# A GRU's hidden product, made block by block inside an earlier sort instead of in the GRU stage

## The reference

```python
feat_in, feat_out = h @ W_in.T + b_in, h @ W_out.T + b_out
a_in = seg_mean(feat_in[src], dst, N)
a_out = seg_mean(feat_out[dst], src, N)
a = concatenate((a_in, a_out), axis=1)
gi, gh = a @ w_ih.T + b_ih, h @ w_hh.T + b_hh     # 3 x 128 columns each: r, z, n
r, z = sigmoid(i_r + h_r), sigmoid(i_z + h_z)
n = tanh(i_n + r * h_n)
h = (1 - z) * n + z * h
x = layernorm(x + h)
```

## Time and profile before

| | |
|---|---|
| median of 3 runs | 14506.02 us |
| lowest and highest | 14486.2, 14518.42 us |
| the profiled execution: its time | 14487.43 us |
| the profiled execution: its span | 14485.9 us |
| mean granted TensorE clock | 0.815 |
| busy share of the span | TensorE 73%, VectorE 52%, ScalarE 27%, GpSimd 68% |
| stage `sort_records` | from 2371 to 6585 us |
| first loop of `node_update` | from 8777 to 9119 us |

### The profile page before, as it was taken

One profiled execution on the slowest core, in us unless ns is written; L12 is line 12 of the kernel. 1 busy time (PEld: TensorE's weight loads), 2 busy tenths in 40 slices (PEclk: granted clock), 3 DMA queues, 4 the chain that ended last, 5 costly groups with the idle time before them and its releaser, 6 DMA issues. The chain is left out here.

```text
span 14485.9 us, 317356 instructions
## 1 busy us (share of the span) xinstructions
PE 10556.1 (73%) x72077; PEld 8423.3 (58%) x72078; DVE 7488.2 (52%) x28446; ACT 3839.8 (27%) x10046; POOL 9837.9 (68%) x10445
## 2 busy tenths in 40 slices
PE   3666665666666666666777768689999999999961
PEld 2444444555555555555777765467777767777751
DVE  5444444333333333336777765356656656556644
ACT  0000001222222222220000004355555555555530
POOL 4777775777777777777777770267777767777740
PEclk8555556777787777788999989599999999999975
DMA  6722222333333333336777771133333353333351
GB/s 202 273 55 55 55 55 70 107 106 107 107 106 107 106 107 106 107 106 163 187 188 189 188 166 38 34 73 79 80 80 80 80 71 80 80 80 79 80 47 31
DMA packets 2182961, 1488.42 MB, mean 103 GB/s; under 512 B 1344360, under 2 KB 1972744, under 8 KB 2181125
## 3 DMA queue, kind: packets, MB, share of 16 engines
q0 software_dynamic: 387600, 800.47, 20.4%
q1 hardware_dynamic: 1751242, 565.87, 17.1%
q10 hardware_dynamic: 43942, 120.50, 2.3%
HBM read 1117.42 MB, written 480.14 MB: 110 GB/s over the span
## 5 line engine op out<-in xcount | busy, mean ns | idle before, releaser
L1637 POOL DMA_INDIRECT ring<-q_rows,small x3556 | 3360.4, 945 | 1205.2 <-issue 927.9
L992 POOL DMA_INDIRECT edges_a<-ring,small x1664 | 1596.8, 960 | 586.6 <-issue 505.7
L992 POOL DMA_INDIRECT edges_b<-ring,small x1664 | 1596.5, 959 | 507.1 <-issue 504.4
L1124 POOL DMA_INDIRECT ring<-in_x,ring x1664 | 1570.2, 944 | 536.9 <-issue 522.9
L746 POOL DMA_INDIRECT ring<-in_x,ring x1664 | 1570.0, 944 | 530.2 <-issue 487.6
L1677 PE MATMUL bank<-w,ring 64*128 64x129 f32 x7112 | 1743.3, 325 | 127.6 <-DVE ring L1591 105.6
L784 PE MATMUL bank<-ring 128*128 128x129 f32 x3328 | 1281.2, 492 | 758.1 <-DMA ring<-in_x,ring 546.7
L784 PEld LDWEIGHTS bank<-ring 128*128 128x128 f32 x3328 | 827.7, 310 | 1177.3 <-DMA ring<-in_x,ring 585.0
L923 PE MATMUL bank<-ident_b,ring 128*128 128x128 bf16 x3332 | 422.1, 266 | 1480.8 <-DVE ring L878 1480.8
L947 PE MATMUL bank<-p,ring 128*128 x6656 | 1347.0, 366 | 128.3 <-ACT ring L977 80.7
L1677 PEld LDWEIGHTS bank<-w,ring 64*128 64x128 f32 x7112 | 1057.1, 186 | 639.7 <-DVE ring L1591 312.1
(11 more groups left out here) (253 smaller groups left out, 21022.0 us busy)
## 6 DMA issues: line engine op xcount, KB each, us to landing
p<-edges_b SPq DMA_DIRECT2D x525, 262.0 KB
p<-edges_a SPq DMA_DIRECT2D x520, 262.0 KB
ring<-bonds_by_dst SPq DMA_DIRECT2D x3344, 32.0 KB
bonds_by_dst<-in_bond ACTq DMA_DIRECT2D x5, 20625.0 KB, 159.8
ring<-edges_a SPq DMA_DIRECT2D x1792, 33.0 KB
ring<-edges_b SPq DMA_DIRECT2D x1776, 33.0 KB
ring<-q_rows,small POOLq DMA_INDIRECT x3556
ring<-in_x,ring POOLq DMA_INDIRECT x3328
```

The lines of the kernel that those rows point to most:

```text
L992: pool.indirect_dma_start(out=c.edges[s], out_offset=bass.IndirectOffsetOnAxis(ap=pos[:, k:k + 1], axis=0), in_=rec[:, k, :], in_offset=No ...
L1124: pool.indirect_dma_start(out=gath[:, at, 0:D], out_offset=None, in_=c.ins["x"], in_offset=bass.IndirectOffsetOnAxis(ap=ids[g][:, 0, k:k + ...
L1637: pool.indirect_dma_start(out=gath[:, k, 0:D], out_offset=None, in_=c.q_dram, in_offset=bass.IndirectOffsetOnAxis(ap=gidx[g][:, k % HALF:k ...
```

## The change

In turn i of the sort, for i under 98, block i of x is loaded, transposed (TensorE, after quad 2), copied (ScalarE, after quad 3), multiplied by W_hh with the candidate's bias added (TensorE, after quad 4), copied (ScalarE, after quad 6) and stored to memory as 384 columns (SyncE, in group 3 of the turn). In `node_update` the transpose of x, its two products and the `cand` banks go. The stored rows are loaded with x, VectorE adds 256 of their columns to the bank in a new `sum_rz`, the sigmoid reads that sum, and t1 reads the other 128.

```diff
+    s_xb, s_xt, s_xtc, s_hx, s_hxc, s_hxo = (c.sem("r_x_block_in"), c.sem("r_x_turned"), c.sem("r_x_turned_copied"),
...
+    T_X, A_XT, T_HX, A_HX = 2, 3, 4, 6
...
+            def store_hidden(b):
+                sp.wait_ge(s_hxc, b + 1)
+                sp.dma_start(c.hx_dram[bass.ds(b * P, P), :], hx).then_inc(s_hxo, 16)
+
+            def load_x(b):
+                sp.wait_ge(s_xt, b)
+                sp.dma_start(xb, c.x_pad[bass.ds(b * P, P), :]).then_inc(s_xb, 16)
+
+            load_x(0)
+            per = TURNS_R // SPARTS
+            for part, first, last in ((0, 0, per), (1, per, 2 * per), (2, 2 * per, 3 * per), (3, 3 * per, NB - 1),
+                                      (4, NB - 1, NB), (4, NB, TURNS_R)):
+                if 1 <= part < SPARTS:
...
+                with sp.Fori(first, last) as i:
                     for g in range(GRPS):
                         u = i * GRPS + g
+                        if first < NB and g == GRPS - 1:
+                            store_hidden(i)
+                        if first < NB - 1 and g == GRPS - 1:
+                            load_x(i + 1)
                         sp.wait_ge(s_xv, u * 4 + 3)
...
+            def turn_x(b):
+                pe.wait_ge(s_xb, 16 * b + 16)
+                pe.wait_ge(s_xtc, b)
+                nc.tensor.transpose(xt_bank, xb, c.ident).then_inc(s_xt, 1)
+
+            def hidden(b):
+                pe.wait_ge(s_xtc, b + 1)
+                pe.wait_ge(s_hxc, b)
+                nc.tensor.matmul(hx_bank, xt, c.weight(W_HH, 3 * D), start=True, stop=False, skip_group_check=True)
+                nc.tensor.matmul(hx_bank[:, 2 * D:3 * D], c.ones_f[0:1, :], c.rows[0:1, (B_HH + 2) * D:(B_HH + 3) * D],
+                                 start=False, stop=True, skip_group_check=True).then_inc(s_hx, 1)
+
+            pe.wait_ge(c.s_w, 15 * 16)
...
+                for first, last in ((0, TURNS_R // 2),) if s == 0 else ((TURNS_R // 2, NB), (NB, TURNS_R)):
+                    with pe.Fori(first, last) as i:
...
+                            if first < NB and q == T_X:
+                                turn_x(i)
+                            if first < NB and q == T_HX:
+                                hidden(i)
...
+            def copy_x(b):
+                act.wait_ge(s_xt, b + 1)
+                act.wait_ge(s_hx, b)
+                nc.scalar.copy(xt, xt_bank).then_inc(s_xtc, 1)
+
+            def copy_hidden(b):
+                act.wait_ge(s_hx, b + 1)
+                act.wait_ge(s_hxo, 16 * b)
+                nc.scalar.copy(hx, hx_bank).then_inc(s_hxc, 1)
...
+            for first, last in ((0, NB), (NB, TURNS_R)):
...
+                        if first < NB and q == A_XT:
+                            copy_x(i)
+                        if first < NB and q == A_HX:
+                            copy_hidden(i)
...
     xs = [place(D) for _ in range(XSLOTS)]
+    hxs = [c.spare[:, n * 3 * D:(n + 1) * 3 * D] for n in range(XSLOTS)]
     m_in, m_out = ([place(D) for _ in range(2)] for _ in range(2))
-    m_t = [place(3 * P) for _ in range(2)]
+    m_t = [place(2 * P) for _ in range(2)]
+    rz_pre = [place(2 * D) for _ in range(2)]
...
+                sp.dma_start(hxs[n], c.hx_dram[n * P:(n + 1) * P, :]).then_inc(s_in[n], 16)
...
+                sp.dma_start(hxs[j % XSLOTS], c.hx_dram[bass.ds((b + XSLOTS) * P, P), :]).then_inc(s_in[j % XSLOTS], 16)
...
-                n, b, x = j % 2, i * TURN + j, xs[j % XSLOTS]
+                n, b, x, hidden = j % 2, i * TURN + j, xs[j % XSLOTS], hxs[j % XSLOTS]
...
-                step.link(nc.vector.tensor_tensor(t1, cand[n][:, 0:D], rz[n][:, 0:D], ALU.mult))
+                step.link(nc.vector.tensor_tensor(t1, hidden[:, 2 * D:3 * D], rz[n][:, 0:D], ALU.mult))
...
+            def sum_rz(b, j):
+                n = j % 2
+                dve.wait_ge(s_gate, b + 3)
+                dve.wait_ge(s_in[j % XSLOTS], (b - j) // TURN * 64 + 32 * (j // XSLOTS + 1) if isinstance(b, int)
+                            else rz_turn * 64 + 32 * (j // XSLOTS + 1))
+                nc.vector.tensor_tensor(rz_pre[n], gates[n][:, 0:2 * D], hxs[j % XSLOTS][:, 0:2 * D], ALU.add).then_inc(s_rz, 1)
+
+            sum_rz(0, 0)
             with dve.Fori(0, TURNS_N - 1) as i:
                 step.loop(i, 5 * TURN)
                 for j in range(TURN):
+                    rz_turn = i + (j + 1) // TURN
+                    sum_rz(i * TURN + (j + 1), (j + 1) % TURN)
                     gru(i, j)
             step.end(TURNS_N - 1)
             for j in range(TURN):
+                if j + 1 < TURN:
+                    sum_rz((TURNS_N - 1) * TURN + j + 1, j + 1)
                 gru(TURNS_N - 1, j)
...
-                pe.wait_ge(s_in[j % XSLOTS], i * 32 + 16 * (j // XSLOTS + 1))
...
-                nc.tensor.transpose(turned[n][:, 2 * P:3 * P], xs[j % XSLOTS], c.ident)
...
-                in_t, out_t, x_t = (m_t[n][:, k * P:(k + 1) * P] for k in range(3))
+                in_t, out_t = (m_t[n][:, k * P:(k + 1) * P] for k in range(2))
                 nc.tensor.matmul(gates[n][:, 0:3 * D], in_t, c.weight(W_IH1, 3 * D), start=True, stop=False,
                                  skip_group_check=True)
                 nc.tensor.matmul(gates[n][:, 0:3 * D], out_t, c.weight(W_IH2, 3 * D), start=False, stop=False,
                                  skip_group_check=True)
-                nc.tensor.matmul(gates[n][:, 0:2 * D], x_t, c.weight(W_HH, 2 * D), start=False, stop=False,
-                                 skip_group_check=True)
                 nc.tensor.matmul(gates[n][:, 0:3 * D], has_t[n], rows9[:, 0:3 * D], start=False, stop=True,
-                                 skip_group_check=True)
-                nc.tensor.matmul(cand[n][:, 0:D], x_t, c.weight(W_HH + 2), start=True, stop=False)
-                nc.tensor.matmul(cand[n][:, 0:D], has_t[n], rows9[:, 3 * D:4 * D], start=False,
-                                 stop=True).then_inc(s_gate, 1)
+                                 skip_group_check=True).then_inc(s_gate, 1)
 
...
-                nc.scalar.copy(m_t[n], turned[n][:, 0:3 * P]).then_inc(s_tc, 1)
+                nc.scalar.copy(m_t[n], turned[n][:, 0:2 * P]).then_inc(s_tc, 1)
...
-                act.wait_ge(s_gate, b + 3)
-                nc.scalar.activation(rz[n], gates[n][:, 0:2 * D], ACT.Sigmoid).then_inc(s_sig, 1)
+                act.wait_ge(s_rz, b + 1)
+                nc.scalar.activation(rz[n], rz_pre[n], ACT.Sigmoid).then_inc(s_sig, 1)
```

More of the change, by code:

```diff
@@ L183, in __init__ @@
         self.q_dram = dram("q_rows", [NPAD, D])
+        self.hx_dram = dram("hidden_gates", [NPAD, 3 * D])
         self.s_copy = [nc.alloc_semaphore(f"bonds_copied{k}") for k in range(COPIES)]
@@ L805, in sort_records @@
     QUADS, BK1, TURNS_R = DEEP // QUAD, NB + 1, SLOTS // DEEP
+    s_xb, s_xt, s_xtc, s_hx, s_hxc, s_hxo = (c.sem("r_x_block_in"), c.sem("r_x_turned"), c.sem("r_x_turned_copied"),
+                                             c.sem("r_hidden"), c.sem("r_hidden_copied"), c.sem("r_hidden_out"))
+    T_X, A_XT, T_HX, A_HX = 2, 3, 4, 6
     rec = c.part(0, DEEP * REC).rearrange("p (k r) -> p k r", k=DEEP)
@@ L818, in sort_records @@
     junk = c.part(top, QUAD * BK1).rearrange("p (k b) -> p k b", k=QUAD)
-    assert top + QUAD * BK1 <= RINGW
+    top += QUAD * BK1
+    xb, xt, hx = c.part(top, D), c.part(top + D, P), c.part(top + 2 * D, 3 * D)
+    assert top + 5 * D <= RINGW
+    xt_bank, hx_bank = c.bank[5][:, 0:P], c.bank[6][:, 0:3 * D]
     posf = c.small[:, 64:64 + DEEP].rearrange("p (q j) -> p q j", j=QUAD)
@@ L851, in _ @@
                 load_bonds(g, g, 0)
-            for part in range(SPARTS):
-                if part:
+            def store_hidden(b):
[9 more added lines that the diff above has]
+                if 1 <= part < SPARTS:
                     sp.wait_ge(c.s_copy[part + 1], 16)
-                with sp.Fori(part * (TURNS_R // SPARTS), (part + 1) * (TURNS_R // SPARTS)) as i:
+                with sp.Fori(first, last) as i:
                     for g in range(GRPS):
                         u = i * GRPS + g
+                        if first < NB and g == GRPS - 1:
+                            store_hidden(i)
+                        if first < NB - 1 and g == GRPS - 1:
+                            load_x(i + 1)
                         sp.wait_ge(s_xv, u * 4 + 3)
@@ L867, in _ @@
             sp.wait_ge(s_tab, 64)
+            sp.wait_ge(s_hxo, 16 * NB)
         @block.vector
@@ L955, in _ @@
                                  start=True, stop=False, skip_group_check=True)
[L956 to L961, removed]
+                for first, last in ((0, TURNS_R // 2),) if s == 0 else ((TURNS_R // 2, NB), (NB, TURNS_R)):
+                    with pe.Fori(first, last) as i:
+                        for q in range(QUADS):
+                            rank(i, q)
+                            turn_hot(i + (q + 1) // QUADS, (q + 1) % QUADS)
+                            find(i, q)
```

(28 more changed lines are left out.)

## The result

| | before | after |
|---|---|---|
| median | 14500.44 us (4 runs) | 14781.56 us (4 runs) |
| lowest to highest | 14486.2 to 14518.42 | 14779.64 to 14793.73 |
| span of the profiled execution | 14485.9 | 14778.7 |

The ratio is 1.0195, with a 95% interval of 1.0177 to 1.0213: the change makes the kernel 281 us slower.

The account below looks back on a forecast made before the run. GpSimd's scatters were taken to bound the sort, TensorE the GRU blocks. Profiled 14487.4 us + 271 (GRU loop) + 3 (stage start) + 0 (sort) = 14761; as a median, 18.6 us higher, 14780 us; range 14615 to 14830.

Parts of the forecast that it names:

- What left TensorE: GRU blocks: a transpose and three products go, 1.21 us a block; 119 us only if TensorE stayed the bound.
- The chain: GRU blocks: each tanh waits for the one before through ScalarE, TensorE and VectorE; 4.70 us at full clock, 6.49 at lower.
- The clock: GRU blocks: TensorE's granted clock falls from 1.00 to a mean of 0.57, placed nearer 0.50 than 0.79.
- The rival with the full clock: GRU blocks: the same chain at full clock, 4.70 us a block, +130 us, a median of 14636; 17%.
- the blend of the two clocks: GRU blocks: a seventh of the time at 4.70 us a block, the rest at 6.49, giving 6.2 us.
- The table load: GRU loop: in each of six turns one activation table load of 1.28 us lies on the chain, 8 us in all.
- The 3 us for the start: Start of the GRU stage: seven more loads and a second round of TensorE work ahead of the first tanh, +3 us.
- The sort at nothing: Sort: the added work costs 0 us, covered by the ring of eight quads with about 28 us of lead.
- My bound of +15: Sort: upper bound of +15 us for the fill of the first turn and stray stalls.
- TensorE's share of it: Sort: the added transpose and products make TensorE about 170 us more busy.
- TensorE stays the bound: GRU stage: TensorE still sets the length and the kernel gets faster, -119 us, to 14387; 5%.

Follow-up runs that it names:

- e2: The changed kernel with four idle bf16 products of 512 columns behind each block's gates on TensorE; 14652.52 us, ratio 1.0104 to the kernel before.
- e3: The changed kernel with TensorE's gates of block b ahead of the transposes of b+1; 14544.31 us, ratio 1.0031 to the kernel before.
- e1: The change's sort with the GRU stage of the kernel before, so the hidden product is made twice; 14497.09 us, ratio 1.000 to the kernel before.
- e4: The changed kernel with VectorE's addition for block b+1 moved behind keep of block b; 14492.08 us, ratio 0.9995 to the kernel before.
- e9: The kernel of e6 (addition behind y) run again on another chip; 14439.84 us, ratio 0.9970 to the kernel before.
- e5: The changed kernel with VectorE's addition for block b+1 behind the statistics of block b; GRU loop 368.5 us, 3.80 a block.
- e6: The changed kernel with VectorE's addition for block b+1 behind y of block b; GRU loop 291.4 us, 3.00 a block.

## Why the prediction was right

**The total**: 14780 was forecast, 14781.6 measured. That it came so near is luck: against the profiled execution 274 us more were said and 292.8 measured, 19 too few, and 18.6 us were added because the profiled execution lay that far under the median of three, which in the kernel after it did by 1.3 (14780.24 against 14781.56).

**What left TensorE** (1.21 us a block, 119 in all) left it and was worth nothing, as said: the stage had become a chain.

**The chain** was read rightly, link by link: the waits of the profile after name L1460, L1504 and t2. At the full clock it was worked out as 4.70 us and is 4.73 (e2's median interval); without scalings and transposes 3.6, and 3.61 (e3). At the lower clock 6.49, and the most frequent interval of the kernel after is 6.56 to 6.57. That the loss lies in this chain and not in the sort is shown by e1 and e4.

**The clock** was placed at 0.57 and is 0.56, and e2 shows that its fall is worth some 126 us. That it fell was argued from busy shares, and these don't settle it. In e3 the same loop was at 0.50 while TensorE was 81% busy, in its rhythm of 5.15 us, and at 1.00 while it was 65% busy, in that of 3.61:

```profile
8860.00:8880.00 20.00, 16.12 (x31) 6.48 (x31) 8.82 (x35) 6.48 (x24) 0.00 (x0) 0.50 0.18 52
8890.00:8910.00 20.00, 12.95 (x46) 5.63 (x44) 12.91 (x50) 8.19 (x31) 0.00 (x0) 1.00 0.28 79
```

The same products take about twice as long at the lower level (L1456 1.44 us to the next start, where it was 0.75), so a low clock itself makes the share high. The direction was well argued from the second loop's 0.50; that the place between 0.50 and 0.79 came out to 0.01 is in part luck. The Trainium skill's rule (TensorE: Matmul & The Clock Gate, "Why this matters for your kernels"), by which a loop without long gaps keeps its clock, did not hold here: TensorE's idle stretches are 2.4 to 2.5 us in the rows above, and the clock was 0.53 to 0.59 in every 100 us of the stage. The second loop of the kernel before speaks the same way, at 0.50 with this idle stretch:

```profile
9202.07 0.47 PE L1410 MATMUL bank<-consts,ring 128*128 128x128 f32 x1 [1.31 <-DVE ring L1318]
```

The rival with the full clock had 14636.

**What was a little off**: the loop grew by 291 us where 271 was said. 6.2 us a block was taken, 6.39 is the mean outside the turns' first blocks. The chain explains at most 0.07 of these 0.19: a block all at the lower clock takes 6.56 us (9194.91 to 9201.47) where 6.49 was said, 4.17 of it TensorE's against 4.13. The larger part, and the term that was mis-sized, is the blend of the two clocks. I let a seventh of the time be made of blocks of 4.70 us. But the clock changes within a block, and most of the time at the upper level fell where TensorE idled and had nothing to speed up; here an idle stretch, then the products behind it:

```profile
9206.67:9209.07 2.40, 0.01 (x1) 0.00 (x0) 1.86 (x7) 1.37 (x6) 0.00 (x0) 1.00 0.00 0
9209.61:9212.97 3.36, 3.36 (x6) 1.27 (x5) 0.17 (x1) 0.00 (x0) 0.00 (x0) 0.51 0.27 78
```

Summed over windows like the first, the idle stretches ahead of L1438 are 237 us and hold 52 us at the upper level, of some 75 in the whole loop. One interval of 97 is 4.73 us. The table load cost about 1.7 us a turn, not 1.28: the turn's first interval is 8.25 against 6.56. The 3 us for the start were 1.5: the stage itself began 5.2 us later (8763.5 against 8758.2 for its first load), 2.4 of it from the sort's first scatter on. Between the loop and the end 5 us came back, which I have not traced.

**The sort at nothing** was right: e1 at 1.000. My bound of +15 wasn't needed. TensorE's share of it was put too high, about 170 us for a measured 114.

**The rivals**: the full clock (17%) was e2's case, not the kernel's. That TensorE stays the bound (5%) was false for this order. With the addition moved 41 of the 119 us are had (e9), and there VectorE's queue sets the length, not TensorE. I had named the place, `sum_rz`, but not that moving it decides the sign.

**In e4's expectation** the failed step was to count only what stands between the addition and the tanh. An operation that waits in VectorE's queue delays everything behind it, and `drop` and y stood there too: 44 us of waiting for TensorE in the 300 from 8790 to 9090.

## What to carry to other kernels

Where an operation consumes the *next* block's product, put it behind everything of this block that others wait for: VectorE's queue turned a wait for the next block into a wait of this one. But leave something between it and what waits for its result: directly ahead of the next t1 (e5) it cost 3.80 us a block, behind y 3.00 (e6). Follow who is waited for until the circle closes, and divide its length by the number of blocks that it spans; here one operation's place made that number one or two, worth 287 us (e4), and 323 with the place behind y (e9), each against the kernel before on the same chip. And when work is taken from TensorE, ask what its clock will be afterwards, since the rest of its work may double with it, as L1456 did here (0.75 to 1.45 us).

## What was not expected of the hardware

Products that compute nothing made two loops faster: by 133 us (625.2 to 491.8) where TensorE had been 62% busy, with the clock going from 0.56 to 0.93, and by 31 us where it had been 58% busy (0.50 to 0.98). And in e3 one loop ran in two rhythms, 3.61 and 5.15 us, with the same instructions, at a clock of 1.00 and 0.50. Eight of the nine long intervals stand at the start of the loop or follow a turn's first interval, in which a table is loaded; that the chain and its clock hold each other in either rhythm fits this, but no run tests it.
